# Router logits of a recurrence stage computed by column quarters of the array, with the tokens as the moved operand

## The chip, the cores and the metric

The kernel runs on one core of one Trainium2 chip. The metric is the device time of one execution in microseconds (us), the median of three. The engines have short names in the profile: PE is TensorE's matmul side and PEld its weight load, DVE is VectorE, ACT is ScalarE, POOL is GpSimd, and SP is SyncE, which starts most of the DMAs. L12 is line 12 of the kernel before.

## The reference, cut to what matters

The model is two layers over x of 16 batches x 256 tokens x 512 channels. The part that concerns this case is the first layer: a recurrence over time (wkv), a residual, a layer norm, and then a mixture of eight experts plus one shared expert. The router scores and the gate of the shared expert are one small product with nine output columns.

```
x = x + tanh(g_xattn[0]) * wkv(w, u, layernorm(x), ctx)      # recurrence
xf = layernorm(x)
scores = xf @ gate_w.T                 # 8 experts, 512 channels contracted
ew, ei = top_k(scores, 2);  ew = softmax(ew)
routed = sum over the 2 chosen experts of ew * expert(xf)
shared = silu(xf @ sh_gate.T) * (xf @ sh_up.T) @ sh_down.T
x = x + tanh(g_ffn[0]) * (routed + sigmoid(xf @ se_gate_w.T) * shared)
```

The second layer (attention and 64 experts) follows and is not touched.

## The kernel before

`wkv_phase` is the first large stage. It works on one batch of 256 tokens per turn, 16 turns, and each engine has its own program with a hand-written order; engines meet only in semaphores. A turn is a software pipeline over three batches: in the same turn the engines run the recurrence of batch `b`, the residual, norm, router and the first three quarters of the shared expert's gate/up product of the batch before it (`one`), and the last gate/up quarter, the down product and the scatter of routing entries of the batch two before (`two`). Turns 3 to 14 (of 0 to 15) are a hardware loop of two turns per round.

On PE a turn is, in this order: `gate_up(two, 3)` (L515), `post_y(one)` (L491: transposes of the recurrence's result yT), `down(two)` (L533), `post_xn(one)` (L499: transposes of the normed tokens into PSUM), `logits(one)` (L507), `gate_up(one, 0)`, `pre(after)` (L481), `gate_up(one, 1)`, `ranks(one)` (L524: counts of tokens per expert, which wait for DVE's `chosen`), `gate_up(one, 2)`.

`logits` multiplies xnT (channels on partitions, 4 blocks of 128, 256 tokens) by the router weights `wr`. Before, the tokens stand in the array (128 columns) and the nine columns of `wr` are moved: for each half of the tokens (`TJ` = 2) four blocks of channels (`KC` = 4) are accumulated. The result has tokens on partitions, which is the form that DVE's `route` reads.

On DVE a turn is: `hidden(two, 3)`, `residual` (L746) and norm statistics of `one`, the statistics of the next batch, a scan (L713), the denominator, `slots(two)` (L783 to L805), a second scan (L724), `shared(two, 0)` (L820), `bonus_values` (L729), `shared(two, 1)`, `route(one)` (L756 to L777: copy of the logits, top two, one-hot of the chosen experts), `hidden(one, 0)` (L812, L816), the first half of a reciprocal (L734), `hidden(one, 1)`, the second half, `quotient` (L740: makes yT), `hidden(one, 2)`. `gate_up(one, 0)` may start when `shared(two, 0)` has read its PSUM bank (semaphore `freed`), and `hidden(one, n)` waits for ACT's tanh of gate n (L607), which waits for `gate_up(one, n)`.

POOL works on SBUF tensors: norm constants (L299 to L304), four indirect DMAs of `scatter` (L670), `numerator` (L662), `undrift` (L649, which waits for ACT's copies of `pre`, L572) and `values` (L656).

## Time and profile before

| what | value |
|---|---|
| time, median of 3 runs | 2361.86 us (2357.37 to 2371.07) |
| span of the profiled execution | 2397.4 us |
| PE busy over the span | 2035.5 us, 85% |
| DVE busy over the span | 1293.9 us, 54% |
| ACT, POOL busy over the span | 747.7 us, 867.9 us |
| recurrence stage (about 10 to 533 us of the span) | 523 us |

The profiled execution is a run of its own. Its span is what the rows are measured in; no other time is given for it. It lies 35.5 us above the median of the timed runs, so a change worked out from the rows is added to the median, not to the span. In the rows of stretches the columns are: stretch and its length, busy us (and instructions) of PE, PEld, DVE, ACT and POOL, the granted clock as a share of 2.4 GHz, DMA share, GB/s. A PE row with xN counts hardware passes: a float32 matmul leaves two records, so the eight matmuls of `logits` are sixteen records. Start times are from the span's start. "idle before <- releaser" tells what ended the engine's idle time ahead of a row.

### The profile page before, as it was taken

How to read it: one execution, taken by the hardware profiler on the slowest of the kernel's cores; microseconds unless marked ns; L12 is line 12 of the kernel's file. 1: busy time of each engine (PE TensorE's matmuls, PEld its weight loads, DVE VectorE, ACT ScalarE, POOL GpSimd, SP SyncE). 2: the span in 40 equal slices, each digit the busy share in tenths (PEclk: the TensorE clock that was granted, in tenths of full speed). 3: DMA queues.
4: the chain of work that ended last, by engine and by line, in shares of the span. 5: the costliest groups of instructions: out<-in, count | busy, mean ns of one | idle time of the engine just before them, and what ended most of it. 6: DMA issues, size and time to landing. Idle time of an engine off the chain costs nothing. (4 is left out here: it accounts for less than half of the span.)

```text
span 2397.4 us, 39219 instructions
## 1 busy us (share of the span) xinstructions
PE 2035.5 (85%) x11962; PEld 1459.7 (61%) x11963; DVE 1293.9 (54%) x3012; ACT 747.7 (31%) x2176; POOL 867.9 (36%) x839
## 2 busy tenths in 40 slices
PE   2999999994699999569999999999998778878886
PEld 1766777773577777357777777777776543333332
DVE  5888888863344444237766766666666522211221
ACT  2333223312222222254544444445454211111110
POOL 5555555533333333143333333334333222211111
PEclk9999999987899999679999999999999989888888
DMA  6432222231133333321111111122112249999996
GB/s 222 141 88 86 81 88 88 70 115 49 53 102 105 97 100 102 128 88 62 63 63 62 61 62 62 67 95 84 62 62 91 91 154 358 352 349 352 357 354 182
DMA packets 129901, 314.56 MB, mean 131 GB/s; under 512 B 33346, under 2 KB 41538, under 8 KB 121604
## 3 DMA queue, kind: packets, MB, share of 16 engines
q1 hardware_dynamic: 102772, 260.64, 31.4%
q0 software_dynamic: 26880, 52.68, 7.8%
q8 instruction: 43, 0.70, 0.1%
q14 instruction: 62, 0.51, 0.1%
q10 hardware_dynamic: 144, 0.03, 0.0%
HBM read 253.13 MB, written 62.33 MB: 132 GB/s over the span
## 5 line engine op out<-in xcount | busy, mean ns | idle before, releaser
L1543 ACT ACTIVATE attn_pr<-attn_score_ps,attn_nmax 128x128 f32<-128x128 f32 x496 | 201.5, 418 | 205.4 <-DVE attn_nmax L1696 202.4
L327 PE MATMUL attn_ffn_ps<-attn_xnT_high,attn_wgu_high 128*128 128x256 f32 x704 | 211.4, 300 | 13.4 <-DVE attn_hT_low L1788 11.5
L1654 POOL DMA_INDIRECT list<-attn_pair,attn_pos x192 | 191.9, 999 | 80.5 <-issue 61.2
L327 PE MATMUL attn_ffn_ps<-attn_xnT_high,attn_wgu_low 128*128 128x256 f32 x704 | 202.1, 287 | 3.6 <-issue 3.6
L327 PE MATMUL attn_ffn_ps<-attn_xnT_low,attn_wgu_high 128*128 128x256 f32 x704 | 202.2, 287 | 2.5 <-issue 2.3
L299 POOL TENSOR_SCALAR attn_norm_var_eps<-attn_norm_mean_var 128x2 f32<-128x2 f32 x32 | 7.9, 247 | 505.2 <-DVE attn_norm_mean_var L293 505.1
L1941 POOL DMA_INDIRECT out<-routed_ym,routed_place x32 | 50.2, 1569 | 342.7 <-DVE routed_ym L2104 292.2
L1696 DVE TENSOR_REDUCE attn_nmax<-attn_score_ps 128x2 f32<-128x256 f32 x248 | 126.3, 550 | 86.2 <-PE attn_score_ps L1385 59.9
L988 POOL DMA_INDIRECT y<-routed_ys,first_ffn_pair x72 | 74.0, 1027 | 229.2 <-DVE routed_ys L1138 226.2
L327 PE MATMUL routed_gu_ps<-routed_wgu_high,routed_xT_high 128*128 x288 | 126.1, 438 | 35.9 <-POOL first_ffn_wgu_low L945 35.9
L327 PEld LDWEIGHTS attn_ffn_ps<-attn_xnT_high,attn_wgu_high 128*128 128x128 f32 x704 | 138.1, 196 | 26.1 <-DVE attn_hT_low L1788 16.1
L515 PE MATMUL wkv_ffn_ps<-wkv_xnT,wkv_wg 128*128 128x256 f32 x512 | 147.9, 440 | 4.0 <-DVE wkv_x L820 4.0
L1395 PE MATMUL attn_tr_ps<-ident,attn_pr 128*128 128x128 f32 x768 | 117.4, 292 | 37.0 <-ACT attn_pr L1543 36.6
L327 PEld LDWEIGHTS attn_ffn_ps<-attn_xnT_high,attn_wgu_low 128*128 128x128 f32 x704 | 137.6, 195 | 4.0 <-issue 4.0
L327 PEld LDWEIGHTS attn_ffn_ps<-attn_xnT_low,attn_wgu_high 128*128 128x128 f32 x704 | 138.1, 196 | 1.3 <-issue 1.2
L2104 DVE COPY routed_ym<-routed_merged_ps 128x512 f32<-128x512 f32 x32 | 22.1, 691 | 195.9 <-PE routed_merged_ps L2019 195.9
L1395 PEld LDWEIGHTS attn_tr_ps<-ident,attn_pr 128*128 128x128 f32 x768 | 88.1, 147 | 59.2 <-issue 49.4
L1701 DVE COPY second_ffn_room<-attn_tr_ps 128x384 f32<-128x384 f32 x96 | 52.9, 551 | 131.4 <-PE attn_tr_ps L1395 98.7
L515 PE MATMUL wkv_ffn_ps<-wkv_xnT,wkv_wu 128*128 128x256 f32 x512 | 123.8, 385 | 0.0
L515 PEld LDWEIGHTS wkv_ffn_ps<-wkv_xnT,wkv_wg 128*128 128x128 f32 x512 | 109.4, 221 | 21.3 <-DVE wkv_x L820 4.7
L1382 PE MATMUL attn_score_ps<-second_ffn_room 32*128 32x256 f32 x992 | 118.8, 358 | 0.7 <-issue 0.7
L327 PE MATMUL routed_gu_ps<-first_ffn_wgu_low,routed_xT_high 128*128 x288 | 119.2, 414 | 0.0
(287 smaller groups left out, 5163.0 us busy)
## 6 DMA issues: line engine op xcount, KB each, us to landing
second_ffn_room<-in_w_gu SPq DMA_DIRECT2D x32, 1408.0 KB
routed_wgu_a<-in_w_gu SPq DMA_DIRECT2D x16, 1408.0 KB
routed_wgu_b<-in_w_gu SPq DMA_DIRECT2D x16, 1408.0 KB
wkv_x<-in_x SPq DMA_DIRECT2D x32, 512.0 KB, 3.8
second_ffn_room<-y SPq DMA_DIRECT2D x32, 512.0 KB
second_ffn_room<-in_w_down SPq DMA_DIRECT2D x32, 512.0 KB
wkv_vT<-in_ctxT SPq DMA_DIRECT2D x16, 512.0 KB, 4.2
xn<-wkv_xn SPq DMA_DIRECT2D x16, 512.0 KB, 2.8
```

The source lines that it names most:

```text
L299: nc.gpsimd.tensor_scalar(self.var[:], self.mv[:, :, 1], EPS, None, ALU.add).then_inc(self.rstd_s, 1)
L327: ins = nc.tensor.matmul(out, a[i], b[j], start=start and n == 0, stop=stop and n == 2)
L515: ins = nc.tensor.matmul(ffn_ps[n % 2][:, col:col + T], w[:, k, n * P:(n + 1) * P], xnT[:, k, :], start=(k == 0), stop=(k == KC - 1))
L988: nc.gpsimd.indirect_dma_start(io["y0"], bass.IndirectOffsetOnAxis(ap=pair[t.s][:, 1:2].bitcast(U32), axis=0), ys[t.s % SLOTS0][:], None, ...
L1382: nc.tensor.matmul(score_ps[:, a, KEYS[j]], qT[b.s][r:r + D, k, j * P:(j + 1) * P], kT[b.s][r:r + D, k, 0:(j + 1) * P], start=(j == 1), st ...
L1395: ins = nc.tensor.transpose(tr_ps[bank][:, col * P:(col + 1) * P], pr[u % 2][:, z // 3, z % 3, :], c.ident[:])
L1543: nc.scalar.activation(pr[u % 2][:, a, j:2 * j + 1, :].rearrange("p k t -> p (k t)"), score_ps[:, a, KEYS[j]], ACT.Exp, bias=nmax[u % 2][: ...
L1654: nc.gpsimd.indirect_dma_start(io["list1"], bass.IndirectOffsetOnAxis(ap=pos[b.s][:, j, k:k + 1], axis=0), pair[b.s][:, j, k, :], None, bo ...
L1696: v.tensor_reduce(nmax[u % 2][:, :, j], score_ps[:, :, KEYS[j]], AX.X, ALU.max, negate=True).then_inc(max_s, 1)
L1701: v.tensor_copy(prT[u % 4][:, 0].rearrange("p k t -> p (k t)"), tr_ps[0][:, 0:3 * P]).then_inc(tr_ev[0], 1)
L1941: nc.gpsimd.indirect_dma_start(io["out"], bass.IndirectOffsetOnAxis(ap=place[q.s % SLOTS1][:].bitcast(U32), axis=0), ym[q.s % SLOTS1][:], ...
L2104: v.tensor_copy(ym[q.s % SLOTS1][:], merged_ps[:]).then_inc(ym_s, 1)
```

## The change

The operands of `logits` change places. The router weights of one block of 128 channels, padded with zeros from 9 to 32 columns (`QUARTER`), stand in one quarter of the array's columns, and all 256 tokens are moved through it. The four blocks of channels use the four quarters, so the partial sums of block k land on PSUM partitions 32k to 32k+31, in the half of `route_ps` that was unused. ACT copies this 128x256 block to SBUF (`logits_copy`, into `lgT`). Then PE multiplies it, standing in the array, with a 0/1 matrix `fold` of nine columns (`logits_back`): this adds the four partial sums and turns the result back to tokens on partitions, into the same columns of `route_ps` as before. `logits_back` stands behind `gate_up(one, 0)` in PE's order. `route` still waits for `logit_s`, which `logits_back` now raises. ACT's copy stands between the copies of xnT and the norm of the next batch. At the stage's start POOL clears `wr` (128x128), SP's load of the router weights waits for that, and DVE makes `fold` with one reduction.

```diff
+QUARTER = P // KC
-        wr = m.sb("wr", [P, KC, E0 + 1])
+        wr = m.sb("wr", [P, KC, QUARTER])
+        fold = m.sb("fold", [P, QUARTER])
+        lgT = m.sb("logitsT", [P, T])
...
                 load(FIRST)
+                sp.wait_ge(wr_zero_s, 1)
...
                 def logits(b):
                     pe.wait_ge(xn_ev, 2 * b.i + 2)
                     wait(pe, pair_s, b.i)
-                    for j in range(TJ):
-                        for k in range(KC):
-                            ins = nc.tensor.matmul(route_ps[:, j * (E0 + 1):(j + 1) * (E0 + 1)], xnT[:, k, j * P:(j + 1) * P],
-                                                   wr[:, k, :], start=(k == 0), stop=(k == KC - 1))
+                    for k in range(KC):
+                        ins = nc.tensor.matmul(route_ps[k * QUARTER:(k + 1) * QUARTER, T:2 * T], wr[:, k, :], xnT[:, k, :],
+                                               start=True, stop=True, tile_position=(0, k * QUARTER))
+                    ins.then_inc(lgT_s, 1)
+
+                def logits_back(b):
+
+                    pe.wait_ge(lgT_ev, b.i + 1)
+                    for j in range(TJ):
+                        ins = nc.tensor.matmul(route_ps[:, j * (E0 + 1):(j + 1) * (E0 + 1)], lgT[:, j * P:(j + 1) * P],
+                                               fold[:, 0:E0 + 1], start=True, stop=True)
                     ins.then_inc(logit_s, 1)
...
                         post_xn(one)
                         logits(one)
                         gate_up(one, 0)
+                        logits_back(one)
                     if after:
                         pre(after)
...
+                def logits_copy(b):
+                    act.wait_ge(lgT_s, b.i + 1)
+                    wait(act, logit_s, b.i)
+                    nc.scalar.copy(lgT[:], route_ps[:, T:2 * T]).then_inc(lgT_ev, 1)
...
                         post(b.before())
+                        logits_copy(b.before())
                     if not b.last:
                         norm_pre(b.after())
...
+                nc.gpsimd.memset(wr[:], 0.0).then_inc(wr_zero_s, 1)
...
+                v.tensor_reduce(fold[:], c.ident[:].rearrange("p (k e) -> p e k", k=KC), AX.X, ALU.add).then_inc(fold_s, 1)
```

PE's queue in a turn, from the transposes of xn to the ranks, in the kernel before (route_ps holds the logits, ffn_ps the gate/up banks; the brackets are the semaphores waited for):

```order
L499 MATMUL wkv_post_ps<-ident,wkv_xn 128x128 [waits wkv_norm2_normed_s]
L499 MATMUL wkv_post_ps<-ident,wkv_xn 128x128 x3
L507 MATMUL wkv_route_ps<-wkv_wr,wkv_xnT 128x9 [waits wkv_pairs,wkv_xn_evacuated]
L507 MATMUL wkv_route_ps<-wkv_wr,wkv_xnT 128x9 x7
L515 MATMUL wkv_ffn_ps<-wkv_xnT,wkv_wg 128x256 [waits wkv_ffn_bank_read]
L515 MATMUL wkv_ffn_ps<-wkv_xnT,wkv_wg 128x256 x3
L515 MATMUL wkv_ffn_ps<-wkv_xnT,wkv_wu 128x256 x4
L481 MATMUL wkv_pre_ps<-ident,wkv_k_tok 128x128 [waits wkv_pre_evacuated,setup_gates_broadcast]
```

The same place of PE's queue in the changed kernel (its lines are 5 to 12 higher):

```order
L504 MATMUL wkv_post_ps<-ident,wkv_xn 128x128 [waits wkv_norm2_normed_s]
L504 MATMUL wkv_post_ps<-ident,wkv_xn 128x128 x3
L511 MATMUL wkv_route_ps<-wkv_xnT,wkv_wr 32x256 [waits wkv_pairs,wkv_xn_evacuated]
L511 MATMUL wkv_route_ps<-wkv_xnT,wkv_wr 32x256 x3
L527 MATMUL wkv_ffn_ps<-wkv_xnT,wkv_wg 128x256 [waits wkv_ffn_bank_read]
L527 MATMUL wkv_ffn_ps<-wkv_xnT,wkv_wg 128x256 x3
L527 MATMUL wkv_ffn_ps<-wkv_xnT,wkv_wu 128x256 x4
L519 MATMUL wkv_route_ps<-wkv_fold,wkv_logitsT 128x9 [waits wkv_logits_copied]
L519 MATMUL wkv_route_ps<-wkv_fold,wkv_logitsT 128x9
L486 MATMUL wkv_pre_ps<-ident,wkv_k_tok 128x128 [waits wkv_pre_evacuated,setup_gates_broadcast]
```

Eight matmuls that give the logits ahead of `gate_up(one, 0)` become four ahead of it and two behind it; what DVE's `route` waits for has moved from ahead of the eight matmuls of `gate_up` to behind them.

ACT's queue in a turn around its copies of xnT, in the kernel before:

```order
L599 COPY wkv_xnT<-wkv_post_ps 128x4x128 [waits wkv_xn_transposed,wkv_gate_up]
L599 COPY wkv_xnT<-wkv_post_ps 128x4x128 [waits wkv_xn_transposed]
L310 ACTIVATE wkv_k_tok<-wkv_x,wkv_norm_shift,wkv_norm_rstd 128x512 [waits setup_pool_made,wkv_pre_transposed]
L310 ACTIVATE wkv_k_tok<-wkv_x,wkv_norm_shift,wkv_norm_rstd 128x512
L607 ACTIVATE wkv_tanh_gate<-wkv_ffn_ps 128x256 [waits wkv_gate_up]
```

And in the changed kernel:

```order
L613 COPY wkv_xnT<-wkv_post_ps 128x4x128 [waits wkv_xn_transposed]
L618 COPY wkv_logitsT<-wkv_route_ps 128x256 [waits wkv_logits,wkv_logits_by_channel]
L311 ACTIVATE wkv_k_tok<-wkv_x,wkv_norm_shift,wkv_norm_rstd 128x512 [waits setup_pool_made,wkv_pre_transposed]
L311 ACTIVATE wkv_k_tok<-wkv_x,wkv_norm_shift,wkv_norm_rstd 128x512
L626 ACTIVATE wkv_tanh_gate<-wkv_ffn_ps 128x256 [waits wkv_gate_up]
```

One copy has come in, and the norm of the next batch (k_tok) now stands behind PE's four new matmuls. DVE's and POOL's queues keep their order inside the turns.

## Rows read from the trace of the kernel before

**Rows 1.** Recurrence stage: its length, busy time by engine, clock, DMA.

```profile
10.00:533.00 523.00, 453.05 (x1985) 345.25 (x1986) 418.17 (x840) 151.50 (x304) 289.74 (x240) 0.92 0.35 110
```

**Rows 2.** Timeline of PE through two turns: start us, us, instruction.

```profile
269.91 1.95 PE L507 MATMUL wkv_route_ps<-wkv_wr,wkv_xnT 128*128 128x9 f32 x16 [0.68 <-ACT wkv_xnT L599]
272.45 3.64 PE L515 MATMUL wkv_ffn_ps<-wkv_xnT,wkv_wg 128*128 128x256 f32 x8 [0.59 <-DVE wkv_x L820]
275.88 1.97 PE L515 MATMUL wkv_ffn_ps<-wkv_xnT,wkv_wu 128*128 128x256 f32 x8
...
289.14 1.04 PE L491 MATMUL wkv_post_ps<-ident,wkv_yT 128*128 128x128 f32 x8
...
300.35 3.58 PE L507 MATMUL wkv_route_ps<-wkv_wr,wkv_xnT 128*128 128x9 f32 x16 [0.68 <-ACT wkv_xnT L599]
303.78 3.44 PE L515 MATMUL wkv_ffn_ps<-wkv_xnT,wkv_wg 128*128 128x256 f32 x8
307.06 1.89 PE L515 MATMUL wkv_ffn_ps<-wkv_xnT,wkv_wu 128*128 128x256 f32 x8
...
331.36 1.95 PE L507 MATMUL wkv_route_ps<-wkv_wr,wkv_xnT 128*128 128x9 f32 x16 [0.68 <-ACT wkv_xnT L599]
```

**Rows 3.** Timeline of DVE in the same two turns.

```profile
271.67 0.73 DVE L820 SCALAR_TENSOR_TENSOR wkv_x<-wkv_ffn_ps,wkv_ssc,wkv_x 128x512 f32<-128x512 f32 x1
...
286.80 1.22 DVE L740 TENSOR_TENSOR wkv_yT<-first_ffn_down 128x1020 f32<-128x1020 f32 x1
...
290.55 1.40 DVE L746 SCALAR_TENSOR_TENSOR wkv_x<-wkv_post_ps,gate,wkv_x 128x512 f32<-128x512 f32 x2
...
302.11 0.72 DVE L820 SCALAR_TENSOR_TENSOR wkv_x<-wkv_ffn_ps,wkv_ssc,wkv_x 128x512 f32<-128x512 f32 x1
...
304.54 0.16 DVE L756 COPY wkv_lg<-wkv_route_ps 128x18 f32<-128x18 f32 x1
...
305.99 0.18 DVE L777 TENSOR_TENSOR wkv_chosen<-wkv_hot 128x16 bf16<-128x16 f32 x1
309.40 0.42 DVE L812 SCALAR_TENSOR_TENSOR wkv_silu_gate<-wkv_tanh_gate,wkv_ffn_ps 128x256 f32<-128x256 f32 x1 [3.24 <-ACT wkv_tanh_gate L607]
```

**Rows 4.** Stretches around both logits, as rows 1; 1.00 or 0.50 is the clock.

```profile
269.90:272.60 2.70, 2.10 (x17) 2.02 (x18) 2.70 (x3) 1.37 (x2) 2.25 (x1) 1.00 0.40 149
272.60:276.00 3.40, 3.40 (x9) 2.69 (x10) 3.02 (x14) 0.00 (x0) 2.49 (x4) 0.50 0.24 86
...
299.90:306.80 6.90, 6.45 (x23) 5.91 (x24) 5.99 (x17) 1.81 (x3) 5.09 (x4) 0.51 0.36 134
```

**Rows 5.** Timeline of PE, attention stage: column quarters (128*32), and its fold product.

```profile
1046.67 1.51 PE L1409 MATMUL attn_out_ps<-second_ffn_room 128*32 128x256 f32 x16
...
1052.29 0.41 PE L1409 MATMUL attn_out_ps<-second_ffn_room 128*32 128x256 f32 x2
...
1052.54 0.39 PE L1409 MATMUL attn_out_ps<-attn_prT,second_ffn_room 128*32 128x256 f32 x2
...
1073.27 0.56 PE L1435 MATMUL attn_route_ps<-attn_fold,attn_logitsT 128*128 128x64 f32 x4
```

**Rows 6.** The stretch of the quarters' 1.51 us, as rows 1.

```profile
1046.60:1048.20 1.60, 1.60 (x18) 0.69 (x18) 0.00 (x0) 1.07 (x4) 0.00 (x0) 0.50 0.00 0
```

**Rows 7.** Timeline of POOL and DVE: POOL's products beside DVE's small ones.

```profile
276.90 2.37 POOL L662 TENSOR_TENSOR first_ffn_down<-first_ffn_down 128x1020 f32<-128x1020 f32 x1
279.48 2.36 POOL L649 TENSOR_TENSOR first_ffn_down<-first_ffn_down,wkv_drift 128x1024 f32<-128x1024 f32 x1 [0.21 <-ACT first_ffn_down L572]
...
307.33 2.36 POOL L662 TENSOR_TENSOR first_ffn_down<-first_ffn_down 128x1020 f32<-128x1020 f32 x1
...
489.09 0.18 DVE L756 COPY wkv_lg<-wkv_route_ps 128x18 f32<-128x18 f32 x1 [1.81 <-PE wkv_route_ps L507]
...
490.00 2.35 POOL L662 TENSOR_TENSOR first_ffn_down<-first_ffn_down 128x1020 f32<-128x1020 f32 x1
490.06 2.32 DVE L767 TENSOR_TENSOR wkv_gap<-wkv_top 128x2 f32<-128x2 f32 x1
```

More of the change, by code:

```diff
@@ L393, in wkv_phase @@
         logit_s, chosen_s, rank_s = m.sem("logits"), m.sem("chosen_done"), m.sem("ranks")
+        wr_zero_s, fold_s, lgT_s, lgT_ev = m.sem("router_zeroed"), m.sem("fold_made"), m.sem("logits_by_channel"), m.sem("logits_copied")
         gap_s, tgap_s = m.sem("gap_done"), m.sem("tanh_gap")
@@ L450, in _ @@
                 load(FIRST)
-                for t, name in ((wr[:, :, 0:E0], "gate_w0"), (wr[:, :, E0:], "se_gate"),
+                sp.wait_ge(wr_zero_s, 1)
+                for t, name in ((wr[:, :, 0:E0], "gate_w0"), (wr[:, :, E0:E0 + 1], "se_gate"),
                                 (wg[:], "sh_gate"), (wu[:], "sh_up"), (wd[:], "sh_down")):
@@ L558, in _ @@
                 pe.wait_ge(weights_in, 5 * 16)
+                pe.wait_ge(fold_s, 1)
                 turns(pe, B, lambda b: turn(b, not b.first and b.before(), b.third and b.before().before(), not b.last and b.after()))
@@ L638, in _ @@
                 post(LAST)
+                logits_copy(LAST)
                 tanh_gate(LAST, 0)
```

## The prediction

> **What bounds the kernel now.** I read the stretches by stage first, then the timeline of each engine through two neighbouring turns, and last the granted clock around the logits. The recurrence stage takes 523 us, with PE busy for 453 and DVE for 418 [rows 1]: neither is full, so a turn is a chain that passes from one to the other. The turns come in two kinds that alternate. Logits start at 269.91, 300.35 and 331.36 [rows 2], so the turns last 30.44 and 31.01 us, 30.73 in the mean. I call the first kind B (logits at 269.91) and the second A (300.35). Sixteen batches pass through the stage; the turns at its two ends lack one of the three batches in flight.
>
> In B the sixteen passes of the logits take 1.95 us and end at 271.86, but `gate_up(one, 0)` starts at 272.45, released by DVE's `shared` (L820), which ends at 272.40 [rows 2, 3]. In A the same passes take 3.58 us and `gate_up` follows them directly at 303.78, while `shared` had ended at 302.83 [rows 2, 3]. So the logits hold PE up in every second turn only, by 303.78 - 302.83 = 0.95 us; in the other one they lie beside DVE's second scan. The factor of 1.8 between 1.95 and 3.58 is the clock: 1.00 (2.4 GHz) in the stretch of B's logits, about half (1.2 GHz) in A's [rows 4].
>
> From the end of `gate_up(one, 0)`, which I call G (277.85 in B, 308.95 in A), PE has work without a gap up to `post_y` at 289.14 = G + 11.29. DVE works along the same stretch and has yT ready at 286.80 + 1.22 = 288.02, 1.12 us earlier [rows 2, 3]. This 1.12 us is the whole slack of DVE's chain. Before G DVE is free: in A it has done `route` at 306.17 and waits 3.24 us for the tanh, until 309.40 = G + 0.45 [rows 3]. From `residual` (L746, 290.55 = G + 12.70) the chain goes on through the norm to the next logits; G to next logits is 22.50 us in B and 22.41 in A [rows 2, 3].
>
> **The change part by part.** *The four quarter matmuls.* The attention stage has the same form: four quarters of 32 columns, 256 float32 tokens moved, two passes each. The first pass starts at 1052.29 and the last of the second passes ends at 1052.54 + 0.39 = 1052.93, so eight passes take 0.64 us; sixteen of the mixed widths take 1.51 us at the clock of 0.50 [rows 5, 6], so eight take between 0.75 and 1.51 us there. I take 0.65 and 1.1 us. Both fit into the 2.5 us in which DVE finishes its scan and `shared`: 272.45 - 269.91 = 2.54 in B, 302.83 - 300.35 = 2.48 in A. So `gate_up(one, 0)` starts 2.5 us after the logits in both kinds. That is no gain in B and 0.9 us in A, 0.45 us per turn in the mean.
>
> The Trainium skill ("TensorEngine Tiling (Array Packing)", Key Properties) says that a change of the tiling mode drains TensorE, which speaks against this change: it switches twice per batch. Both switches would lie in the same 2.5 us, so by this rule the sum stays as it is.
>
> *ACT's copy.* It stands before the norm of the next batch (k_tok), whose transposes PE wants only after G, more than 7 us later. It costs nothing while that cover stands; without it its 128x256 elements would be near the 0.42 us of DVE's pass over as many [rows 3].
>
> *The fold product.* Two matmuls, four passes, on PE behind `gate_up(one, 0)`. The four passes of the attention stage's fold take 0.56 us [rows 5]; they overlap their neighbours a little, so I charge 0.5 us (bounds 0.4 and 0.56). It is on the path: PE has no gap between G and `post_y`.
>
> *The later route.* `route` waits for the fold, G + 0.5 at the earliest, and not for the logits. It takes 304.54 to 306.17, 1.63 us [rows 3], so `hidden(one, 0)` starts at G + 2.15 and not G + 0.45: DVE's chain is 1.7 us later. The slack of 1.12 us takes most of it. yT is ready at G + 10.17 + 1.7 = 11.87, and PE itself arrives at 11.29 + 0.5 = 11.79. So both ends tie and the turn's second part grows by 0.5 to 0.6 us; I take 0.55. What is late next is `residual`, and with it the whole norm chain. The `ranks` product, `gate_up(one, 2)` and the tanhs wait for DVE too, but stand later in PE's queue than DVE reaches them, by over 2 us.
>
> *The clock.* `gate_up(one, 0)` takes 5.40 us in B (272.45 to 277.85) and 5.17 in A [rows 2]. In B 3.4 us of it lie at half clock [rows 4], which cost 1.7, so it would be 3.7 us at full clock. With the new form the lull ahead of it is as in B, so I take 5.4, 0.1 above the mean of the two.
>
> *Sum.* Per turn: -0.45 (A's logits) + 0.55 (fold and route) + 0.1 (clock) = +0.2. I add 0.1 for `route` meeting POOL's `numerator` for a moment (below): +0.3, over 13 turns +4 us. At the stage's ends three batches have no `shared` in the way: if their logits are like A's, 3.58 becomes 1.1 us, half of the 2.5 is given back to the clock and 0.5 to 0.7 to fold and route, so I estimate -0.5 each, together -1.5. The start (a clear of `wr`, one small reduction) lies beside the first loads, 0. The sum is +3 us, within the span of 2397.4; the median of the timed runs is 2361.86, and the 3 us are added to that: **2365 us**, no change that can be measured. About 0.5%, 12 us, is what a measurement of this kernel can tell from none.
>
> **The rivals.** *Slower: the later route runs into POOL's products.* In the turn at 490 DVE's `gap` subtraction (L767), two operands of two columns in SBUF, took 2.32 us and not the tenth or two of its neighbours, since POOL's `numerator` (L662) ran from 490.00 for 2.35 us [rows 7]. `route` has three such instructions, the last (`chosen`, L777) 1.45 us after its start [rows 3]. Before, it ended ahead of G: POOL's `numerator` starts at 276.90 = G - 0.95 in B and at G - 1.62 in A, `undrift` at 279.48 = G + 1.63 [rows 7]. Now `route` lies at G + 0.5 to G + 2.15. `numerator` starts 7.0 us after the logits in both kinds (276.90 - 269.91, 307.33 - 300.35) and lasts 2.37, so with G 7.9 us after the logits it ends at G + 1.46, just as L767 comes: that one starts 490.06 - 489.09 = 0.97 us after `route` [rows 7], at G + 1.47. `undrift` moves with the fold to G + 2.1, and `chosen` starts at G + 1.95. The margin is 0.15 us. If the fold is later or the clock is back earlier by more than this, DVE waits a whole `undrift`, 2.36 us, and nothing hides it. One turn in three so: 4 to 5 x 2.36 = +10, with the +3 above 2375. Every turn: 15 x 2.36 + 3 = +38, 2400. For it speaks the thin margin; against it that a turn delayed so starts its `gate_up` elsewhere against the clock's fall, with more of it at half clock, and then has room. I give it 0.31, of which 0.06 is for every turn.
>
> The Trainium skill ("SBUF — State Buffer", Who interferes with whom) says the same as a rule: a DVE instruction with two SBUF inputs and a GpSimd one that reads SBUF exclude each other, and who comes first keeps the ports to its end. By it `chosen` at 1.95 goes through and at 2.15 it pays in full; the trace agrees, with 2.32 us [rows 7].
>
> *Faster: the clock stays high.* The old logits move nine columns per pass and the clock is low right after them in both kinds [rows 4]. The new ones move 256. If these count as work where the old ones did not, the fall before `gate_up(one, 0)` may not come in some turns, and each spared one gives 1.7 us: in half of them -12 + 3, 2353; in all, 15 x 1.7 = -25, 2340. Against it: they last only 0.65 us in a lull of about 5 us. I give 0.13.
>
> *The quarters don't overlap.* Then eight passes take as long as those of `gate_up`, 1.89 us at full clock [rows 2], and 3.8 at half: A's gain is gone, +0.45 x 13 = 6 us more, 2371. The attention stage's rows speak against it; 0.06. The forecast itself has 0.50.
>
> **How the numbers follow.** Likeliest 2365 alone: 2358 to 2371. The cases reach from 2340 to 2400; leaving out the all-turns ends and half a tenth beyond, the range is 2350 to 2383. Faster by over 0.5% (below 2350): most of the clock's second half and a little noise, 0.10. Slower (above 2374): half of the partly blocked case, all of the fully blocked one, some spill, 0.27. Within: 0.63.
>
> **What the profile after would show.** The new logits at 0.6 to 0.7 us at full clock, about 1.1 at half; `gate_up(one, 0)` 2.5 us after them in every turn, released by DVE's L820 and not by PE's own order; four passes of about 0.5 us more behind it; DVE idle from `shared` to G + 0.5 and `route` right behind; `post_y` at G + 11.8; turns of 30.9 to 31.1 us, no longer alternating. The blocked case shows as a `hot` or `chosen` of over 2 us beside `undrift` and single turns of 33 us. The forecast is wrong if these are common, if DVE's chain has a wait that I took for work (then `post_y` is not later), or if the turns fall to 30 us, with `gate_up` at 3.7.

## The result and the profile after

The changed kernel takes 2355.42 us (median of 11 runs, 2349.87 to 2366.45) against 2365.85 for the kernel before (median of 11, 2357.37 to 2377.03). The ratio is 0.9959 with a 95% interval from 0.9942 to 0.9976: 0.4% faster, 5.7 to 13.7 us. I had forecast +3, to 2365 from the 2361.86 us of the first three runs; the median of all eleven is 4 us higher. The profiled execution of the kernel before, at a span of 2397.4 us, was an untypically long one; that of the changed kernel (2353.9) lies beside its median. A second profiled execution of the kernel before has a span of 2367.0, and later comparisons of whole stages use it too.

In the middle of the recurrence stage the changed kernel does nearly what I had said. This is the timeline of PE through one turn (start us, us, instruction); G is now 280.10 + 1.99 = 282.09.

```profile
274.14 0.64 PE L511 MATMUL wkv_route_ps<-wkv_xnT,wkv_wr 128*32 128x256 f32 x8 [0.68 <-ACT wkv_xnT L613]
276.68 3.62 PE L527 MATMUL wkv_ffn_ps<-wkv_xnT,wkv_wg 128*128 128x256 f32 x8 [1.90 <-DVE wkv_x L842]
280.10 1.99 PE L527 MATMUL wkv_ffn_ps<-wkv_xnT,wkv_wu 128*128 128x256 f32 x8
281.93 0.51 PE L519 MATMUL wkv_route_ps<-wkv_fold,wkv_logitsT 128*128 128x9 f32 x4
282.29 1.07 PE L486 MATMUL wkv_pre_ps<-ident,wkv_k_tok 128*128 128x128 f32 x8
...
293.77 1.04 PE L496 MATMUL wkv_post_ps<-ident,wkv_yT 128*128 128x128 f32 x8
...
304.98 0.64 PE L511 MATMUL wkv_route_ps<-wkv_xnT,wkv_wr 128*32 128x256 f32 x8 [0.67 <-ACT wkv_xnT L613]
```

And of DVE in the same turn, with the first and the last instruction of `route`, the first `hidden` and the last piece of the quotient:

```profile
282.47 0.18 DVE L778 COPY wkv_lg<-wkv_route_ps 128x18 f32<-128x18 f32 x1 [4.05 <-PE wkv_route_ps L519]
...
283.94 0.18 DVE L799 TENSOR_TENSOR wkv_chosen<-wkv_hot 128x16 bf16<-128x16 f32 x1
284.03 0.41 DVE L834 SCALAR_TENSOR_TENSOR wkv_silu_gate<-wkv_tanh_gate,wkv_ffn_ps 128x256 f32<-128x256 f32 x1
...
292.17 1.22 DVE L762 TENSOR_TENSOR wkv_yT<-first_ffn_down 128x1020 f32<-128x1020 f32 x1
```

Set beside [rows 2, 3]: eight passes for sixteen, in 0.64 us; `gate_up(one, 0)` 2.54 us behind them, which DVE releases and not PE's order; the fold right behind it; `hidden(one, 0)` at G + 1.94; `post_y` at G + 11.68, where it stood at G + 11.29. The turn lasts 30.84 us, and the next 30.76.

What I had not seen coming is at the stage's end. These are the passes of the 15th and 16th logits and what follows them, first in the kernel before:

```profile
485.47 3.59 PE L507 MATMUL wkv_route_ps<-wkv_wr,wkv_xnT 128*128 128x9 f32 x16 [0.68 <-ACT wkv_xnT L599]
488.90 3.76 PE L515 MATMUL wkv_ffn_ps<-wkv_xnT,wkv_wg 128*128 128x256 f32 x8
492.46 2.90 PE L515 MATMUL wkv_ffn_ps<-wkv_xnT,wkv_wu 128*128 128x256 f32 x8
...
515.33 1.95 PE L507 MATMUL wkv_route_ps<-wkv_wr,wkv_xnT 128*128 128x9 f32 x16 [0.78 <-ACT wkv_xnT L599]
517.14 2.56 PE L515 MATMUL wkv_ffn_ps<-wkv_xnT,wkv_wg 128*128 128x256 f32 x8
519.48 3.04 PE L515 MATMUL wkv_ffn_ps<-wkv_xnT,wkv_wu 128*128 128x256 f32 x8
```

and then in the changed one:

```profile
490.12 0.64 PE L511 MATMUL wkv_route_ps<-wkv_xnT,wkv_wr 128*32 128x256 f32 x8 [0.68 <-ACT wkv_xnT L613]
490.69 1.99 PE L527 MATMUL wkv_ffn_ps<-wkv_xnT,wkv_wg 128*128 128x256 f32 x8
492.52 1.89 PE L527 MATMUL wkv_ffn_ps<-wkv_xnT,wkv_wu 128*128 128x256 f32 x8
...
507.08 1.09 PE L496 MATMUL wkv_post_ps<-ident,wkv_yT 128*128 128x128 f32 x8 [0.79 <-DVE wkv_yT L762]
...
516.70 0.64 PE L511 MATMUL wkv_route_ps<-wkv_xnT,wkv_wr 128*32 128x256 f32 x8 [0.78 <-ACT wkv_xnT L613]
517.27 1.99 PE L527 MATMUL wkv_ffn_ps<-wkv_xnT,wkv_wg 128*128 128x256 f32 x8
519.10 1.89 PE L527 MATMUL wkv_ffn_ps<-wkv_xnT,wkv_wu 128*128 128x256 f32 x8
```

Here no `shared` holds `gate_up` back, so it follows the logits at once. Logits and `gate_up(one, 0)` of the 15th batch took 492.46 + 2.90 - 485.47 = 9.89 us and take 492.52 + 1.89 - 490.12 = 4.29; those of the 16th took 7.19 and take 4.29. Some of the 5.6 and 2.9 us goes to the fold and to waits for DVE (0.79 us ahead of `post_y`): the turn is 3.3 us shorter, the end 2.45. The clock differs too, in the same two stretches (busy times of PE, weight loads, DVE, ACT and POOL, then the granted clock), before:

```profile
485.00:515.00 30.00, 29.08 (x117) 22.39 (x117) 22.17 (x47) 4.44 (x11) 9.84 (x11) 0.84 0.46 156
515.00:540.00 25.00, 24.63 (x101) 18.21 (x101) 10.98 (x49) 1.90 (x6) 5.74 (x6) 0.93 0.30 86
```

and after, where it does not fall at all (it does not in any of the four profiles of whole kernels with the changed stage):

```profile
485.00:515.00 30.00, 26.19 (x118) 17.86 (x117) 25.20 (x61) 6.41 (x13) 12.40 (x13) 1.00 0.40 135
515.00:540.00 25.00, 23.09 (x106) 16.52 (x104) 12.80 (x51) 3.19 (x8) 6.69 (x7) 1.00 0.37 113
```

How much of this is the clock's, the end shows by itself. In a third profile of the kernel before (that of the run with a shifted attention stage, told below) the clock stayed up behind the 16th logits, and `gate_up` takes 3.70 us there for 5.38:

```profile
517.19 1.97 PE L515 MATMUL wkv_ffn_ps<-wkv_xnT,wkv_wg 128*128 128x256 f32 x8
519.00 1.89 PE L515 MATMUL wkv_ffn_ps<-wkv_xnT,wkv_wu 128*128 128x256 f32 x8
```

Its end lasts 22.95 us, against 24.63 with the fall and 22.18 in the changed kernel: 1.7 us of the 2.45 are the clock, 0.8 the shorter logits.

The one turn that is longer is that of the fourth batch, and it is my first rival come true, once. These are DVE's last instruction of `route` and POOL's `undrift` beside it, from two views of the same stretch:

```profile
157.72 2.32 DVE L799 TENSOR_TENSOR wkv_chosen<-wkv_hot 128x16 bf16<-128x16 f32 x1
```

```profile
157.66 2.35 POOL L670 TENSOR_TENSOR first_ffn_down<-first_ffn_down,wkv_drift 128x1024 f32<-128x1024 f32 x1 [0.61 <-ACT first_ffn_down L586]
```

POOL came 0.06 us first, and DVE's 16 columns took 2.32 us. In the other turns of the middle `chosen` starts some 1.46 us behind `route`'s first instruction and 0.17 us ahead of `undrift`; in this one it starts 1.70 us behind it, in all four profiles. The distances between the starts of successive logits, read from the timelines of PE (end: from the 16th logits to the end of the stage's last product), show where the stage's time went. The third row and the last three are experiments told below.

| kernel | turns 1 to 5 | turns 6 to 13 | turn 14 | turn 15 | end |
|---|---|---|---|---|---|
| before | 30.9 30.5 31.0 30.4 31.0 | 30.4 and 31.0 in turn | 31.2 | 29.9 | 24.6 |
| before, second profile | 31.7 31.3 30.4 31.2 30.4 | 30.4 to 31.2 | 31.2 | 29.9 | 24.6 |
| before, attention stage shifted | 30.9 30.6 31.0 30.4 30.4 | 30.4 to 31.3 | 31.2 | 29.9 | 22.95 |
| changed | 30.1 31.3 30.8 33.1 31.4 | 30.7 to 31.2 | 31.4 | 26.6 | 22.2 |
| changed, second profile | 29.3 30.8 30.8 33.2 31.2 | 30.7 to 30.8 | 31.4 | 26.6 | 22.2 |
| a quarter of the old logits | 29.3 31.7 30.5 30.4 30.6 | 30.7 to 30.8 | 31.4 | 27.1 | 21.6 |
| changed, products before and after the logits, fold late | 30.1 32.7 32.7 33.0 32.7 | 32.7 to 32.9 | 33.5 | 29.1 | 23.5 |
| changed, fold early, products | 31.8 29.7 31.4 28.8 28.7 | 28.7 to 28.8 | 29.4 | 26.6 | 23.2 |

### The profile page after: what moved, and what is told of

The parts are those of the page before. It is cut to its first block and busy times, and to the rows that moved or that the text cites. A ratio compares the mean times of both kernels' runs of the same rounds, so it can differ in the third digit from the quotient of the medians.

```text
span 2353.9 us, 39125 instructions
## 1 busy us (share of the span) xinstructions
PE 1996.5 (85%) x11898; PEld 1415.1 (60%) x11899; DVE 1291.5 (55%) x3013; ACT 757.3 (32%) x2192; POOL 868.5 (37%) x840
## 3 DMA queue, kind: packets, MB, share of 16 engines
q1 hardware_dynamic: 102772, 260.64, 31.6%
## 5 line engine op out<-in xcount | busy, mean ns | idle before, releaser
L527 PEld LDWEIGHTS wkv_ffn_ps<-wkv_xnT,wkv_wg 128*128 128x128 f32 x512 | 107.5, 219 | 50.5 <-DVE wkv_x L842 31.3
L328 PE MATMUL routed_gu_ps<-routed_wgu_high,routed_xT_low 128*128 x288 | 118.5, 411 | 0.0
## 6 DMA issues: line engine op xcount, KB each, us to landing
routed_wgu_a<-in_w_gu SPq DMA_DIRECT2D x16, 1408.0 KB, 24.4
second_ffn_room<-in_w_down SPq DMA_DIRECT2D x32, 512.0 KB, 24.4
```

The costliest lines, as they stand in the source:

```text
L328: ins = nc.tensor.matmul(out, a[i], b[j], start=start and n == 0, stop=stop and n == 2)
L527: ins = nc.tensor.matmul(ffn_ps[n % 2][:, col:col + T], w[:, k, n * P:(n + 1) * P], xnT[:, k, :], start=(k == 0), stop=(k == KC - 1))
```

## The experiments

I call the theory G that in the middle of the stage a turn is tied to the fall of the clock ahead of `gate_up(one, 0)`: a change of the chain by some tenths moves the fall against the products, and so how much of them lies at half clock, and not the turn.

### The two kernels again, the fold early, and products in the lulls

*The kernel before, unchanged.* 

> The unchanged kernel before, for a second profile. Theory S (stage unchanged): the recurrence stage ends within 1 us of where it ended before (last gate/up about 533 to 540 us), its turns again alternate between 30.4 and 31.0 us, and the attention stage is shorter than the 952 us of the first profile, since that one was an unusual execution: about 915 to 925 us, total 2355 to 2372. Rival R (stage really shorter in common executions): the recurrence stage takes 8 to 10 us longer here than in the changed kernel, that is turns of 31.4 us and not 30.7.

2368.33 us (ratio 1.0009, 0.9994 to 1.0024) beside the runs of the kernel before. *The changed kernel, unchanged.* 

> The changed kernel as it is, for a second profile beside the first one. Theory S: logits 0.64 us, turns of 30.7 to 30.8 us with at most one or two of 33 us in which a DVE instruction of route waits a whole POOL product; the recurrence stage within 1.5 us of that of the kernel before; the rest of the difference of 0.4% lies in the attention stage. Ratio to before 0.994 to 0.998. Rival R: the recurrence stage is 8 to 10 us shorter than that of e1_before_again.

2358.79 us, ratio 0.9961 (0.9944 to 0.9979). The gain repeats. In these two profiles the recurrence stage ends at 541.65 and 537.95 us, 3.7 us apart: more than theory S allowed and less than half of what rival R wanted.

*The fold early.* The product that turns the logits back is issued ahead of `gate_up(one, 0)` (this run's difference from the changed kernel):

```diff
                         logits(one)
-                        gate_up(one, 0)
                         logits_back(one)
+                        gate_up(one, 0)
```

> logits_back stands ahead of gate_up(one, 0), in the lull in which PE waits for DVE's shared; route gets its logits before DVE is free. Theory G (the clock's fall and rise set the turn): the fold costs nothing, post_y is back at 11.3 us after gate_up's end, 0.5 us saved per turn, but the mean turn stays at 30.6 to 30.8 us, since an earlier start of gate_up only puts more of it under the low clock: stage and total within 3 us of the changed kernel's. Rival P (plain sum): each turn is 0.45 us shorter, 30.35 us, and the kernel 6 to 7 us faster than the changed one, 0.3%.

2355.48 us, 0.9953 (0.9932 to 0.9974). PE's timeline of a turn:

```profile
268.86 1.08 PE L511 MATMUL wkv_route_ps<-wkv_xnT,wkv_wr 128*32 128x256 f32 x8 [0.68 <-ACT wkv_xnT L613]
...
271.40 3.78 PE L527 MATMUL wkv_ffn_ps<-wkv_xnT,wkv_wg 128*128 128x256 f32 x8
274.97 2.15 PE L527 MATMUL wkv_ffn_ps<-wkv_xnT,wkv_wu 128*128 128x256 f32 x8
...
288.41 1.04 PE L496 MATMUL wkv_post_ps<-ident,wkv_yT 128*128 128x128 f32 x8
...
299.62 1.08 PE L511 MATMUL wkv_route_ps<-wkv_xnT,wkv_wr 128*32 128x256 f32 x8 [0.68 <-ACT wkv_xnT L613]
```

`post_y` is back at G + 11.29 (G is 277.12), so the fold is off the path; but `gate_up(one, 0)` has grown from 5.41 to 5.72 us, the logits stand at half clock (1.08), and the turn is 30.76 us, 30.72 in the mean of two. What the chain saved, 0.39 us, the longer `gate_up` took back, 0.31; the mean of the changed kernel's steady turns is 30.80.

*Products in the lulls.* The same, with four extra products of 256 columns per turn into an unused bank: two ahead of the transposes of xn, one behind the logits, one behind the fold.

```diff
+                def keep(times):
+                    for n in range(times):
+                        nc.tensor.matmul(spare_ps[:, 0:T], wg[:, 0, 0:P], xnT[:, 0, :], start=True, stop=True)
...
+                        if two:
+                            keep(2)
                         post_xn(one)
                         logits(one)
+                        keep(1)
+                        logits_back(one)
+                        keep(1)
                         gate_up(one, 0)
-                        logits_back(one)
```

> As e3, and four float32 products of 256 columns are added whose result nobody reads (spare_ps): two between down and post_xn, one behind logits, one behind logits_back, all in time in which PE waits. They add work and compute nothing of the result. Theory G: the clock does not fall ahead of gate_up(one, 0), which then takes 3.7 us and not 5.4; turns of 28.7 to 29.1 us; recurrence stage 24 to 30 us shorter, total about 2330, ratio to before 0.987 to 0.990. Rival P: idle time is idle time, the products change nothing or cost up to 0.5 us per turn: ratio as e3, 0.993 to 0.998.

2339.22 us, ratio 0.9882 (0.9861 to 0.9903): 28 us under the kernel before and 16 under the fold early without the products. PE's timeline:

```profile
262.32 0.64 PE L512 MATMUL wkv_route_ps<-wkv_xnT,wkv_wr 128*32 128x256 f32 x8 [0.68 <-ACT wkv_xnT L623]
262.88 0.70 PE L553 MATMUL wkv_spare_ps<-wkv_xnT,wkv_wg 128*128 128x256 f32 x2
263.45 0.61 PE L520 MATMUL wkv_route_ps<-wkv_fold,wkv_logitsT 128*128 128x9 f32 x4
263.91 0.68 PE L553 MATMUL wkv_spare_ps<-wkv_xnT,wkv_wg 128*128 128x256 f32 x2
264.86 1.99 PE L528 MATMUL wkv_ffn_ps<-wkv_xnT,wkv_wg 128*128 128x256 f32 x8 [0.26 <-DVE wkv_x L852]
266.69 1.89 PE L528 MATMUL wkv_ffn_ps<-wkv_xnT,wkv_wu 128*128 128x256 f32 x8
```

`gate_up(one, 0)` takes 266.69 + 1.89 - 264.86 = 3.72 us, the 3.7 that I had worked out for the full clock, and the steady turns last 28.7 us. The clock's fall costs a turn 5.41 - 3.72 = 1.7 us plus what hangs on it.

### Whose are the 10 us: the attention stage?

From its first to its last product the attention stage, which the change does not touch, took 918.3 us in the second profile of the kernel before (998.3 to 1916.6) and 908.1 in that of the changed kernel (992.6 to 1900.6). The same stretch of it, first of the kernel before:

```profile
1170.00:1846.00 676.00, 635.88 (x5121) 508.78 (x5122) 462.84 (x1165) 336.43 (x1185) 244.77 (x274) 0.97 0.20 70
```

then of the changed one:

```profile
1170.00:1846.00 676.00, 633.80 (x5182) 507.94 (x5180) 472.79 (x1196) 339.30 (x1200) 239.89 (x271) 0.99 0.20 70
```

A clock of 0.97 against 0.99 over 676 us is 676 x 0.02 = 14 us of work at full clock, as large as the whole result. I call it theory P that how often the clock falls in this stage depends on where in time its waits lie, and not on the stage's content. So I filled the two waits of PE after which the clock falls there, in both kernels, and shifted the stage's start, in both.

```diff
+                        if u == UNITS - 2 and not b.first:
+                            wait(pe, tr_ev[0], use(b, u))
+                            keep(tr_ps[0], 5)
                         transpose(b, u)
...
+                            wait(pe, out_ev, GROUPS * b.i)
+                            keep(out_ps, 6)
                             ffn_inputs(b.before())
```

> The kernel before, with eleven extra products of the identity with itself per turn of the attention stage only: six ahead of the transposes of the feed-forward inputs (into the bank of the head outputs, before PE waits there) and five ahead of the seventh unit's transposes. Nothing is left out. Theory P (phase): the attention stage took 918.3 us in the kernel before and 907.9 to 908.1 in the changed one because the granted clock fell in it for 34.0 us against 10 to 14 us, and how often it falls depends on where in a turn PE's two waits of 1.3 and 1.8 us meet the clock's steps. With the waits filled the clock stays at 1.00 from the third turn on and the stage takes 895 to 905 us; the time is 2345 to 2355. Theory C (content: the stage is slower because its code or data lie elsewhere): the products change nothing but cost up to 1 us per turn; attention 918 to 930, time 2365 to 2378.

> The changed kernel with the same eleven products per attention turn. Nothing is left out. Theory P: attention takes 895 to 905 us here too, within 3 us of the kernel before with the same products, so what is left between the two is the recurrence stage's 1 to 4 us alone; time 2342 to 2353, 1 to 5 us under the other. Theory C: the difference of 9 us between the two stays.

Both stages kept their clock: over the same stretch it is 1.00 in both profiles. The stage takes 929.8 and 927.5 us, alike within 3 us as theory P says. But the products stand on the path there: even undisturbed turns grew from 52.6 to 54.7 us, so my size for it was wrong, and both kernels are slower: 2382.76 (1.0056, 1.0036 to 1.0076) and 2374.94 (1.0035, 1.0020 to 1.0050). The ratios differ by 0.0021, 5 us, with intervals that overlap. With the clock kept in the attention stage the two kernels are thus, by the ratios, no further apart than their first halves alone (below).

*The start shifted* by three clears of a tile on DVE (the pad), which the stage's first load waits for:

```diff
+                for n in range(3):
+                    if n:
+                        dve.wait_ge(pad_s, n)
+                    v.memset(hot[:], 0.0).then_inc(pad_s, 1)
...
+                sp.wait_ge(pad_s, 3)
                 load(FIRST)
```

> [...] Nothing is left out. Theory P: the stage's start stands elsewhere against the clock's steps, so the number of low stretches in it changes, and its length with it: anywhere from 905 to 920 us, the median time 2358 to 2370. If starts were scattered from run to run anyway, the shift is lost in them and the median is 2369 to 2371. Theory C: attention 918 us as before, the time that of before plus the pad, 2370.

> The changed kernel with the same three clears ahead of the attention stage. Nothing is left out. Theory P with a start that decides: the stage leaves its 908 us, by up to +10, and the median moves from 2357 to between 2359 and 2370. With scattered starts: 2359 to 2361. Theory C: attention stays at 908 and the time is 2360.

2374.44 (1.0021, 1.0004 to 1.0038) and 2359.95 (0.9961, 0.9941 to 0.9980). In the profiles PE's gap ahead of the stage grew by 2.2 and 3.3 us, and the stage took 912.1 and 903.4 us. Counting all profiles in which the stage's own work is untouched, it took 952.2, 918.3, 912.1 and 911.5 beside old logits and 907.9, 908.1, 903.4 beside the changed stage, 910.0, 912.5 and 916.6 in variants of it (fold early without and with products, fold twice): there is no clear step between them. The shift did not settle whether the start decides: 2374.44 lies above all that I had expected, 7 us over the kernel before beside it, but this has 2.2 us of clears in it and an interval from 1 to 9; the changed kernel moved by 1.

### The first half alone

To leave that out I cut both kernels behind the first routed stage; they copy the hidden state to the output.

```diff
-            for phase in (attention_phase, routed1_phase):
-                phase(nc, io, c)
...
+                    sp.dma_start(io["out"][0:N, :], io["x2"][:]).then_inc(out_s, 16)
```

> The kernel before without its attention stage and its last stage: after the first routed stage the hidden state is copied to the output. It is there for the comparison with the next kernel, which lacks the same two stages. About 1010 to 1050 us; PE's recurrence work ends at 538 to 542 us.

> The changed kernel without the attention stage and the last stage, in the same way. Theory S (the recurrence stage gives all of the 9 us): 8 to 10 us under the kernel before it. Theory R (the recurrence stage gives only what its profiles show, 3 us in the mean of four profiles of each, and the rest comes from the granted clock in the untouched attention stage): 2 to 5 us under it.

1012.22 us (1010.12 to 1013.38, 5 runs) and 1006.38 (1005.96 to 1011.17, 6 runs; five of them at most 1007.4): 5.8 us, between the two theories. The first half alone gives over half of the measured 10 us, and the lower end of that interval is 5.7. What is left for the attention stage, some 4 us, can't be told from nothing. The one run at 1011.17 is the profiled one, and its profile says why: turns of 32.6, 33.7, 32.9 and 32.2 us at the start, three of them with a DVE instruction of `route` beside a product of POOL (2.37, 2.34 and 4.08 us).

### What decides in the recurrence stage

*The old logits with the products* (two ahead of the transposes of xn, one behind the logits):

> The kernel before, with its old sixteen-pass logits, and three extra products into an unused bank per turn of the recurrence stage: two of 256 columns ahead of the transposes of xn, one behind the logits. Nothing is left out. Theory G (the turn is locked to the clock's fall, and what the change does to PE's queue hardly matters beside it): the clock stays at 1.00, gate_up(one, 0) takes 3.7 us, turns last 28.7 to 29.2 us instead of 30.7, and the time is 2367 - 14 x 1.7 = 2340 to 2347. Rival: only the new form of the logits (256 columns per pass) keeps the clock up together with the extra products; here it falls as before, and the time is 2367 to 2375.

2354.09 us, 0.9948 (0.9931 to 0.9966), a gain between the two sizes. PE's timeline has turns of both sorts, 30.4 us with the fall and 28.7 without:

```profile
237.40 1.95 PE L508 MATMUL wkv_route_ps<-wkv_wr,wkv_xnT 128*128 128x9 f32 x16 [0.68 <-ACT wkv_xnT L608]
239.94 3.03 PE L516 MATMUL wkv_ffn_ps<-wkv_xnT,wkv_wg 128*128 128x256 f32 x8
...
267.76 1.95 PE L508 MATMUL wkv_route_ps<-wkv_wr,wkv_xnT 128*128 128x9 f32 x16 [0.67 <-ACT wkv_xnT L608]
270.30 1.99 PE L516 MATMUL wkv_ffn_ps<-wkv_xnT,wkv_wg 128*128 128x256 f32 x8
```

Both theories missed: the clock stayed up in three of thirteen turns only. This run had one product fewer than the one of 28.7 us, so it does not tell whether the old form or the smaller number is to blame.

*The fold twice*, eight passes for four behind `gate_up(one, 0)`:

```diff
+                    for again in range(2):
                         for j in range(TJ):
                             ins = nc.tensor.matmul(route_ps[...], lgT[...], fold[:, 0:E0 + 1], start=True, stop=True)
```

> The changed kernel with the product that turns the logits back done twice (eight passes for four), right behind gate_up(one, 0). Nothing is left out. My prediction's sum: the second part of each turn grows by another 0.45 to 0.5 us, and DVE's route starts that much later: turns of 31.2 to 31.3 us, +6 to +7 us, 2364 to 2366. Theory G (lock): the turn stays at 30.7 to 30.8 us and the later logits only move the fall of the clock against gate_up, time within 2 us of the changed kernel; or, if route now meets POOL's undrift in every turn, turns of 33 us and 2385 to 2395.

2374.54 us, 1.0034 (1.0019 to 1.0048), 0.0073 above the 0.9961 of the changed kernel, 17 us. Turns lasted 34.9 and 32.7, then 31.2, 30.9, 32.6 and 31.6 in cycles, 31.6 in the mean: more than my sum, and much more than the tie allows. So the tie works on one side only. A chain that is shorter is held at 30.7 us; one that is longer lengthens the turn. Two of the turns are blocked by POOL (`chosen` 2.33 us at 159.0, `gap` 3.62 at 190.2). The cycle of the others is `gate_up(one, 0)`: it takes 5.36, 5.10, 6.71 and 5.79 us in the turns of 31.2, 30.9, 32.6 and 31.6, and what is left of each turn is 25.8 to 25.9 us. In the changed kernel that rest is 30.84 - 5.41 = 25.4, so the second fold costs 0.4 us a turn, near my sum, and the rest of the growth is a `gate_up` of 5.7 us in the mean, more of which lies at half clock.

*The clock at the end alone*, in the kernel before without its second half, the three products only where no next batch is loaded:

```diff
+                        if two and not after:
+                            keep(2)
                         post_xn(one)
                         logits(one)
+                        if not after:
+                            keep(1)
```

> The kernel before without its attention stage and its last stage (the hidden state is copied to the output), with the three extra products (two ahead of the transposes of xn, one behind the logits) in the last two turns of the recurrence stage only. To be set beside the 1012.2 us of the kernel before and the 1006.4 us of the changed one in the same shortened form. If the changed kernel's gain at the stage's end is the clock alone, that stays up through the last two turns: 3 to 5 us less, 1007 to 1009 us, and the turn from the 15th to the 16th logits falls from 29.9 to about 27. If the gain there is the four-quarter form itself (its passes, its free PE), the extra products bring nothing, 1012 to 1014.

1010.92 us (5 runs, 1009.14 to 1013.42), against 1012.22 (1010.12 to 1013.38): the runs overlap, and neither theory's time came. The stretch of the 15th batch still holds one fall behind the logits,

```profile
489.80:493.20 3.40, 3.40 (x10) 2.66 (x9) 1.31 (x11) 0.00 (x0) 2.96 (x3) 0.50 0.47 160
```

and turn 15 and the end took 28.5 and 23.4 us, 2.7 less than the 29.9 and 24.6 of the same cut kernel without the products. So in this profile about half of the 5.7 us comes with the clock alone, what the extra products cost included; the timed runs show 1.3 us, no clear difference.

*A quarter of the old logits*, the first channel block alone, four passes for sixteen:

```diff
-                        for k in range(KC):
+                        for k in range(1):
```

> The kernel before in the same shortened form, with logits over the first of the four channel blocks alone: four passes for sixteen. It leaves out three quarters of the router's product. My prediction's term: every second turn gains 0.95 us, 0.45 in the mean, and the ends gain too: 1012.2 - 13 x 0.45 - 3 = 1003 to 1004, with steady turns of 30.3. Theory G (the clock's fall takes it back, since a shorter chain meets it with a longer gate_up): steady turns stay at 30.7 us, and only the ends gain: 1008 to 1012.

1003.06 us (1002.62 to 1005.57), 9 us less. That is the time of my prediction's plain sum and not the 1008 to 1012 of theory G, but the turns are not those of the sum. Steady turns:

```profile
271.09 1.02 PE L507 MATMUL wkv_route_ps<-wkv_wr,wkv_xnT 128*128 128x9 f32 x4 [0.68 <-ACT wkv_xnT L599]
273.63 3.78 PE L515 MATMUL wkv_ffn_ps<-wkv_xnT,wkv_wg 128*128 128x256 f32 x8 [1.52 <-DVE wkv_x L820]
277.20 2.17 PE L515 MATMUL wkv_ffn_ps<-wkv_xnT,wkv_wu 128*128 128x256 f32 x8
...
301.87 1.02 PE L507 MATMUL wkv_route_ps<-wkv_wr,wkv_xnT 128*128 128x9 f32 x4 [0.67 <-ACT wkv_xnT L599]
```

`gate_up(one, 0)` takes 5.74 us here and 5.7 in every steady turn, where it took 5.40 and 5.17 in turn [rows 2], and the turn is 30.78 us. The gain of 0.95 us in every second turn is real in PE's queue and wholly given back: from the logits' start to G it is 2.54 + 5.74 = 8.28 us, and 8.27 in the mean of the two kinds before. This is theory G's turn, in a kernel without any fold. The time comes from the ends: turn 15 and the end take 27.1 and 21.6 us, together 5.8 less. (The first turn is 2.4 us shorter, but the first logits come 2.7 later.) The profiles' spans differ by 6.0 us; what the other 3 of the timed 9 us are is open. In turn 15 the clock still falls here, and the turn is 2.8 us shorter all the same, so there the short logits count in full without it:

```profile
486.78 1.02 PE L507 MATMUL wkv_route_ps<-wkv_wr,wkv_xnT 128*128 128x9 f32 x4 [0.67 <-ACT wkv_xnT L599]
487.65 3.76 PE L515 MATMUL wkv_ffn_ps<-wkv_xnT,wkv_wg 128*128 128x256 f32 x8
491.21 2.68 PE L515 MATMUL wkv_ffn_ps<-wkv_xnT,wkv_wu 128*128 128x256 f32 x8
```

*The meeting with POOL made common*: the changed kernel, cut, with the fold late and five extra products (two ahead of the transposes, three behind the logits).

> The changed kernel in the shortened form, with the logits turned back behind gate_up(one, 0) as in the change, and five extra products per turn (two ahead of the transposes of xn, three behind the logits). With the clock at 1.00 gate_up(one, 0) takes 3.7 us and G comes 1.7 us earlier, while POOL's numerator keeps its distance of 7.0 us from the logits. If the meeting with POOL costs what I priced (2.3 us for a DVE instruction beside a product of POOL), the turns are 30 to 32.8 us in spite of the faster gate_up, and the time is 1003 to 1035. If it costs nothing, turns of 28.9 to 29.2 us and 980 to 985.

1035.25 us (1034.75 to 1035.66), 29 us above the cut changed kernel. `gate_up(one, 0)` is at 3.72 us, and every steady turn lasts 32.7 to 33.0. DVE in one of them, and POOL beside it:

```profile
289.27 4.05 DVE L798 TENSOR_TENSOR wkv_gap<-wkv_top 128x2 f32<-128x2 f32 x1
```

```profile
288.64 2.36 POOL L692 TENSOR_TENSOR first_ffn_down<-first_ffn_down 128x1020 f32<-128x1020 f32 x1
290.94 2.35 POOL L679 TENSOR_TENSOR first_ffn_down<-first_ffn_down,wkv_drift 128x1024 f32<-128x1024 f32 x1
```

The subtraction of two columns waits for `numerator` and then for `undrift` behind it: 4.05 us, not the 2.3 that I had priced; `gap` takes 3.84 to 4.08 us in thirteen turns. That is most of the step from the 28.7 us of the kernel with an early fold to 32.8. *The fold early, cut:*

> The changed kernel in the shortened form, with the logits turned back ahead of gate_up(one, 0), as in an earlier run of the whole kernel. The route then ends ahead of POOL's products in every turn. If blocked turns eat part of the changed kernel's gain, this is 2 to 4 us under its 1006.4: 1002 to 1005. If the clock takes everything back, 1005 to 1008.

1007.70 us (1007.43 to 1008.02). No turn of the middle is blocked, and from the third on all last 30.7 to 30.8. It is not faster than the cut changed kernel; the 1.3 us between them are not more than the kernel before differed between the two sets of runs (2366.49 and 2367.58). Its turn 15 and end take 27.9 and 24.4 us, 3.5 more: the fold, which waits for ACT's copy, stands ahead of `gate_up` there, which starts 2.44 and 1.60 us behind the logits and not 0.57, and the clock falls again. One `chosen` at 489.93 takes 3.03 us, to the end of POOL's `numerator`, although that starts later, at 490.56; the same instruction does this in the whole kernel with an early fold. POOL was issuing a transfer when it started; why it waited is open.

## Why the prediction was wrong

**The quarter matmuls** were right: 0.64 us at full clock, 1.08 at half (0.65 and 1.1 said), and no sign of a cost for the change of form (in the 15th batch `gate_up` starts 0.57 us behind the first quarter pass); both lie under DVE's scan, as said. `gate_up(one, 0)` starts 2.54 us behind them and takes 5.41 (5.4 said). **ACT's copy** cost nothing.

**The fold and the later route** were of the right kind and a bit too dear. I charged 0.5 us for the fold and a tie with DVE, together 0.55; `post_y` moved from G + 11.29 to G + 11.68, 0.39, since the next product overlaps the fold, which starts 0.36 us ahead of it. Route starts at G + 0.38, `hidden` at G + 1.94 (2.15 said), and yT is ready 0.4 us before PE wants it. The steady turns are 30.8 us where I had 31.0; before, 30.7. So a steady turn is as good as unchanged, by the two things that I set against each other. From the second to the 15th logits the changed stage takes 403.8 us and the old one 400.3 (means of four profiles each): +3.5, near the +4 that I had for these thirteen turns, but by luck, since 2.3 of it is the one blocked turn. That the gain of 0.45 there would have been lost even without a fold, I did not know; a quarter of the old logits shows it.

**The rival of the blocked route** came, in one turn of fifteen, the same one in all four profiles of whole kernels with the changed stage, +2.3 us. The margin that I had put at 0.15 us is 0.17: in the turn at 282 `chosen` starts at 283.94 and `undrift` at 284.11. In the blocked turn `route` itself is 0.24 us slower up to `chosen`, 1.70 for 1.46, and the margin is gone; why it is slower there is not known. The rule of the Trainium skill ("SBUF — State Buffer", Who interferes with whom), that who comes first keeps the ports, is what the blocked turn's rows show; that a waiting DVE instruction can lose to two products in a row, no row of before had told. The 3.03 us of the early fold, where DVE came first, are not explained.

**The rival of the clock that stays high** did not come in the steady turns: `gate_up(one, 0)` takes 5.4 us there and not 3.7. It came in the last two batches, 3.72 us in each. That the time lies near this rival's 2353 is chance.

**The step that failed is the sum's term for the ends**, "half of the 2.5 is given back to the clock and 0.5 to 0.7 to fold and route, so I estimate -0.5 each, together -1.5". I carried the tie to the clock from the middle of the stage to its end. There the logits stand directly ahead of `gate_up` on PE, and what they save is not given back: turn 15 and the end are 3.3 and 2.45 us shorter, together 5.7, and 5.3 in the mean of four profiles each, as the old end once kept its clock. Part is the short logits alone (2.8 us in turn 15 with a quarter of the old ones, under a clock that falls), part the clock (1.7 us at the end); why it stays up behind the new logits is not shown. At the start the second logits come 1.2 us earlier. So the ends gave 6.5 us where I had 1.5, and this turns the sign. (My sum was loose as well: 13 x 0.3 - 1.5 is +2.4, not +3.) With the middle's +3.5 the stage is 3.0 us shorter in the mean of four profiles each (538.3 to 542.2 us to its last product before, 536.5 to 538.9 after), and the cut kernels are 5.8 us apart. Why those give more than the profiles is open; single executions of either kernel differ by as much.

The remaining 4 us of the difference, if they are real, lie behind the first half, likeliest in the attention stage, whose clock was 0.97 in one profile and 0.99 in another. The times of the whole kernels spread over 16 to 20 us, those of the cut ones over 1 to 5; that the change makes the clock fall less often there was not shown.

## What to carry to other kernels

Where a lull on TensorE comes once per turn and the granted clock falls in it, price a shortening of the chain by what the clock leaves of it, and look at the first and last turns by themselves: a gain may be nil in the middle and real at the ends. A few unused products in the lull can be worth more than the change itself (16 us here, between two kernels with an early fold), but only where PE waits anyway; in the attention stage they cost 2 us a turn. And a clock that stays up moves every meeting with the other engines: with a late fold five such products cost 29 us. When a small DVE instruction is moved, set its place against POOL's large ones with their jitter, and count each POOL product that follows at once.

## What was unexpected of the hardware

With the products in the lulls (fold early) the clock is 1.00 from 190 to 480 us, where it is 0.94 in the changed kernel, and the same sixteen passes of `gate_up(one, 0)` take 3.72 us for 5.41. A chain that is some 0.4 us shorter leaves the turn at 30.7 us, in two different kernels (fold early, a quarter of the old logits), while one that is 0.4 us longer makes it 0.8 us longer (fold twice). A DVE subtraction of two columns took 4.05 us beside two POOL products of 2.36 and 2.35 us.
